# A selective-scan recurrence on one core: softplus' remainder summed on TensorE, one table set for Ln and Exp, six GpSimd drives for seven

## What is computed

```python
dt = softplus(x_dbl[..., :dt_rank] @ W_dt.T + b_dt)      # (B, 1024, 128)
A = -exp(A_log)                                          # (128, 16)
def step(h, inp):
    dt_t, B_t, C_t, u_t = inp
    dA = exp(dt_t[..., None] * A)
    h = dA * h + (dt_t * u_t)[..., None] * B_t[:, None, :]
    return h, einsum('bdn,bn->bd', h, C_t)
y = ys + u * D_skip
return y * silu(z) @ W_out.T
```

## Time and profile before

| what | us |
|---|---|
| median of the three runs | 741.99 |
| lowest and highest run | 741.06, 745.93 |
| span of the profiled execution, first to last instruction | 740.9 |
| median less that span | 1.1 |
| the units, from the first drive to the last product | 45.0 to 473.0 |

### The profile page before, as it was taken

The page is one execution under the profiler, slowest core; times in us unless marked ns, Lnnn a source line. Parts: engine busy times, 40 slices in busy tenths (PEclk is TensorE's granted clock), DMA queues, the critical chain, the costliest instruction groups (busy, mean ns, idle before and its releaser), DMA issues.

```text
span 740.9 us, 10581 instructions
## 1 busy us (share of the span) xinstructions
PE 605.2 (82%) x3591; PEld 253.3 (34%) x3591; DVE 571.3 (77%) x589; ACT 440.8 (59%) x662; POOL 470.9 (64%) x250
## 2 busy tenths in 40 slices
PE   4876696797896787987777788898889988999997
PEld 2321121121221211221212122245656335777762
DVE  4489999998998998998998999554465545666645
ACT  3887767668587578578577555163545515555532
POOL 6369999999999999999999999650000310000002
PEclk9999789789998998998998999999999999999999
DMA  3389566577576666666675675000000000000001
GB/s 99 85 275 306 227 230 234 199 254 236 201 256 233 210 243 237 223 232 229 207 260 198 242 244 199 21 0 1 3 4 9 1 19 1 2 1 2 2 2 60
DMA packets 33112, 105.35 MB, mean 142 GB/s; under 512 B 6933, under 2 KB 7454, under 8 KB 33054
## 3 DMA queue, kind: packets, MB, share of 16 engines
q1 hardware_dynamic: 31958, 103.94, 41.1%
q10 hardware_dynamic: 776, 0.55, 0.3%
q0 software_dynamic: 320, 0.13, 0.1%
HBM read 98.84 MB, written 2.10 MB: 136 GB/s over the span
## 4 chain that ended last, share of the span: by engine, by line
PE 41%; POOL 16%; DVE 16%; issue 15%; ACT 7%; DMA 3%; DVEq 0%; SPq 0%; POOLq 0%; ACTq 0%
POOL hc L1764 8%; POOL dbu L1775 8%; DVE hh_all L1464 7%; PE py L229 6%; PE pb L198 6%; PE px L252 5%; PE py L727 5%; DVE pb L1459 4%; DMA cc<-scr 2%; PE pb L939 2%; PE px L754 2%; PE pb L715 1%; PE py L963 1%; PE px L242 1%; DVE yg L1473 1%
## 5 line engine op out<-in xcount | busy, mean ns | idle before, releaser
L1764 POOL TENSOR_TENSOR hc<-hh_all,cc 128x1024 f32<-128x1024 f32 x128 | 300.2, 2390 | 2.4 <-DVE hh_all L1464 1.3
L727 PE MATMUL py<-hc,w_cst 64*64 64x512 f32 x1024 | 153.2, 658 | 26.9 <-POOL hc L1764 17.1
L1464 DVE TENSOR_TENSOR_SCAN hh_all<-da,pb 128x1024 f32<-128x1024 f32 x72 | 164.6, 2286 | 2.5
L1778 POOL TENSOR_TENSOR yg<-w_xs 128x512 f32<-128x512 f32 x10 | 12.6, 1266 | 232.6 <-DVE w_xs L1599 142.8
L1464 DVE TENSOR_TENSOR_SCAN hh_all<-pb,dbu 128x1024 f32<-128x1024 f32 x56 | 127.7, 2280 | 17.4 <-POOL dbu L1775 13.9
L1775 POOL TENSOR_TENSOR dbu<-bb,dtu_all 128x1024 f32<-128x1024 f32 x56 | 133.8, 2389 | 0.0
L715 PE MATMUL pb<-bc,w_sel 128*128 128x512 bf16 x144 | 48.2, 420 | 66.1 <-DVE hh_all L1464 63.6
L1184 ACT ACTIVATE pb<-dt_all,w_aneg 128x1024 f32<-128x1024 f32 x56 | 62.6, 1118 | 58.5 <-DVE hh_all L1464 56.9
L1459 DVE TENSOR_TENSOR pb<-pb,dtu_all 128x1024 f32<-128x1024 f32 x72 | 87.5, 1215 | 1.9 <-DVE dtu_all L1445 0.2
L286 DVE TENSOR_REDUCE gate_all<-pb 128x1 f32<-128x1024 f32 (+7 forms) x64 | 60.4, 985 | 29.6 <-PE pb L208 14.9
L1184 ACT ACTIVATE da<-dt_all,w_aneg 128x1024 f32<-128x1024 f32 x72 | 80.5, 1137 | 0.5
(11 more groups left out here) (291 smaller groups left out, 950.3 us busy)
## 6 DMA issues: line engine op xcount, KB each, us to landing
cc<-scr SPq DMA_DIRECT2D x128, 512.0 KB, 4.5
bb<-scr SPq DMA_DIRECT2D x56, 512.0 KB, 4.8
w_xs<-hc SPq DMA_DIRECT2D x6, 256.0 KB, 4.6
w_xst<-in_x SPq DMA_DIRECT2D x2, 512.0 KB, 5.4
scr<-bcf SPq DMA_DIRECT2D x8, 128.0 KB, 3.8
w_xs<-dt_all SPq DMA_DIRECT2D x4, 256.0 KB, 6.1
w_xs<-dtu_all SPq DMA_DIRECT2D x4, 256.0 KB, 5.8
out<-yg SPq DMA_DIRECT2D x4, 256.0 KB, 2.6
```

The lines of the kernel that those rows point to most:

```text
L727: last = nc.tensor.matmul(py[part(t), half(r)], ident[part(r), part(r)], hc[u % NHC][part(r), half(t)], start=(n == 0), stop=(n == NS - 1) ...
L1464: nc.vector.tensor_tensor_scan(hh[u % NHH][:, :], decay[:, :], drive[:, :], 0.0, ALU.mult, ALU.add).then_inc(scan_done, 1)
L1764: nc.gpsimd.tensor_tensor(hc[u % NHC][:, :], hh[u % NHH][:, :], cc[u % NCC][:, :], ALU.mult).then_inc(hc_done, 1)
```

## The change

The remainder of softplus leaves VectorE for all sequences but the first. For those, ScalarE's Ln no longer overwrites `px[h]`, but goes to `dt`; TensorE adds 1 to -(1+e) by four matmuls of one row by 128 columns of ones, and then adds `dt`, `ex` and `rl` by identity matmuls. Ln waits for ScalarE's own step instead of VectorE's. After the gate at n = 2 ScalarE loads the table set that has both Ln and Exp. One of seven pooled states of each sequence becomes an own state, and the list is spaced anew.

```diff
-        POOLED = (1, 4, 6, 8, 10, 12, 14)
+        POOLED = (1, 4, 7, 9, 12, 14)
...
+        ones = w["sel"][0:1, 0, :]
...
         def pe_dt_add(pe, s, h):
             pe.wait_ge(ln_done, 2 * s + h + 1)
+            if s:
+                for t in range(4):
+                    nc.tensor.matmul(px[h][:, t * 128:t * 128 + 128], ones, ones, start=False, stop=False, skip_group_check=True)
+                nc.tensor.matmul(px[h][:, :], ident, dt[s % 2][:, half(h)], start=False, stop=False, skip_group_check=True)
             nc.tensor.matmul(px[h][:, :], ident, ex[:, half(h)], start=False, stop=False, skip_group_check=True)
             nc.tensor.matmul(px[h][:, :], ident, rl[:, half(h)], start=False, stop=True,
                              skip_group_check=True).then_inc(px_full[h], 1)
...
         def act_ln(act, s, h):
-            act.wait_ge(lost_done, 2 * s + h + 1)
-            nc.scalar.activation(px[h][:, :], px[h][:, :], ACT.Ln, scale=-1.0).then_inc(ln_done, 1)
-
-        def act_dt_out(act, s, h):
-            act.wait_ge(px_full[h], full(s, ADD))
-            atleast(act, scan_done, NS * (s - 1))
+            if s == 0:
+                act.wait_ge(lost_done, h + 1)
+            else:
+                act.wait_ge(one_done, 2 * s + h + 1)
             if s == 1:
                 for v in (4, 6):
                     act.wait_ge(xs_in[v], 32)
+            nc.scalar.activation(dt[s % 2][:, half(h)] if s else px[h][:, :], px[h][:, :], ACT.Ln, scale=-1.0).then_inc(ln_done, 1)
+
+        def act_dt_out(act, s, h):
+            act.wait_ge(px_full[h], full(s, ADD))
             nc.scalar.activation(dt[s % 2][:, half(h)], px[h][:, :], ACT.Copy).then_inc(dt_done, 1)
...
+                if n == 2 and q < LAST:
+                    act.preload_act_table_set("natural_log_exp_and_others")
                 if q == LAST:
                     act_first_pair(act, n)
...
                     if q < LAST:
-                        if n == 9 + h:
-                            dve_lost(dve, q + 1, h)
                         if n == 11 + h:
                             dve_dtu(dve, q + 1, h)
```

## The result

The kernel after takes 753.6 us (median of four runs, 750.5 to 755.8), the kernel before beside it 741.5; the ratio is 1.015, with an interval of 1.011 to 1.018. The forecast was 737.0, the range 727 to 748: the change was to bring a little time, and it costs some.

The account below looks back on a forecast made before the run. GpSimd was taken to set the pace at 53.15 us a sequence; 52.4 after saves 5.2, less 1.2 in sequence 0, plus 0.8 at the end: 4.8 off the 740.9 span, 736.1, median 737, range 727 to 748.

Parts of the forecast that it names:

- GpSimd's part: GpSimd's work per sequence: one drive fewer takes off 2.31 us, leaving 22 x 2.31 = 50.84 us.
- VectorE's part: VectorE's work per sequence: 1.24 us more for the own state, 1.16 less for the remainders, giving 50.43 us.
- The chain to Ln: ScalarE's list from the end of scan 7 to the end of Ln of half 0: 9.1 us.
- The four matmuls of one row: TensorE's four additions with one row of weights and 128 columns: 0.3 us together.
- Half 1: TensorE's additions for the second half of the next dt: 3.24 us, as for half 0.
- The new wait: VectorE's product with u waits for ScalarE's copy: 0.5 us for half 0, 1.1 for half 1, 1.6 a sequence.
- the sum: A sequence takes 50.4 + 0.4 + 1.6 = 52.4 us against 53.15; the units take 419.4 us.
- Half 0 costs 3.24 and is done at 12.4: TensorE's additions for half 0 take 3.24 us and end 12.4 us after scan 7.
- its second rival: TensorE's clock is at half in the additions: at 1.5 us a sequence the time is 747; chance 0.20.
- Sequence 0: Loses 1.2 us: GpSimd's product waits for the C row's DMA, and state 7's drive stands three operations behind.
- GpSimd's drives x48, 54.9 us: Sign in the profile: GpSimd's drives x48, 54.9 us, in place of x56.
- The load at n = 2: ScalarE's added table load: two loads a sequence, not four; their removal taken at nothing more than its place in the chain.

Follow-up runs that it names:

- both_fill: Kernel after, with zero-weight matmuls on TensorE at two places: six ahead of state 8's B row, eight ahead of the wait for half 0's Ln; 738.0 us.
- dt_fill: Kernel after, with six zero-weight matmuls on TensorE ahead of state 8's B row; 741.4 us.
- loads_only: Kernel before, with only the added load at n = 2 of the table set holding Ln and Exp; 744.0 us, ratio 1.001.
- early_no_load: Kernel after, with Ln reading e and the ones, e and relu added ahead of Ln's wait, but without the table load at n = 2; 743.6 us.
- clock_fill: Kernel after, with eight zero-weight matmuls on TensorE ahead of its wait for Ln of half 0; 741.6 us.
- early_old_fill: Kernel after, with additions ahead of Ln's wait, the old list of seven pooled states and eight zero-weight matmuls ahead of half 0's additions; 751.0 us.

## Why the prediction was wrong

**What held.** GpSimd's part: 50.77 us of work (50.84 predicted), idle time before its products instead of waits for its drives, and 50.7 us periods once the chain is hidden. VectorE's part: 50.10 (50.43). The chain to Ln: 9.0 us (9.1) where the projection is not late, without table loads. The four matmuls of one row: 0.32 us (0.3). Half 1: 3.16 (3.24). The new wait: VectorE's product with u for ScalarE's copy, and it decides. With the clock held up at both places (projection and half 0's additions at 1.00 in all seven sequences) the sum held for the units, 419.0 us against 419.4 (both_fill).

**The step that failed** is "Half 0 costs 3.24 and is done at 12.4". It took 4.55 to 4.87 us in six of seven sequences, since TensorE's clock fell from 1.00 to 0.50 on the way. The prediction knew this as its second rival and put it at 0.20, with the argument that TensorE's gaps there would be "1.1, 0.6 and 1.7 us, none as long as 2.4". The 2.4 is the 2.38 us of the earlier trace rows ahead of state 11's B row, where the stretch at 0.50 of the earlier trace rows begins. That fails twice. In sequences 2 to 5 the last gap was 2.25 to 2.74 us. And in sequences 1 and 6 the gaps came out as forecast, and the clock fell all the same, 1.6 and 1.1 us after TensorE had gone back to work. The mistake was to read from two rows of before that gaps shorter than 2.4 us are safe, when the trace of before had seven cases to count. From the first to the last of half 0's two additions, in sequences 1, 2 and 4 (clock in the column before the DMA share):

```profile
132.91:135.81 2.90, 2.90 (x4) 1.11 (x5) 2.87 (x4) 2.07 (x3) 2.90 (x3) 0.65 0.67 216
186.08:188.00 1.92, 1.92 (x4) 0.68 (x4) 1.92 (x3) 1.08 (x2) 1.92 (x2) 0.99 0.67 218
292.47:295.80 3.33, 3.33 (x5) 1.17 (x5) 3.30 (x4) 2.48 (x3) 3.33 (x3) 0.57 0.58 198
```

In the kernel before the clock was already low in half 0's additions in six sequences of seven (2.3 to 3.8 us at a mean of 0.87 to 0.50, instead of 2.0), and it cost nothing there, as GpSimd set the pace (VectorE waited 0.2 us for the copy in all). All seven had a gap of 1.9 to 2.4 us some 3 us ahead, the one at full clock too (2.38): the length of a gap doesn't tell. So 0.20 was far too low for this rival. Its time of 747 adds 1.5 us a sequence. No run shows that term as such, nor the spread whose middle ends the range and whose upper part has the chance of 0.08; what the runs showed in its place is 9.5 us over six sequences in half 0's additions, 1.6 each, so the price was about right. The 747 falls short of the 753.6 by the next point, by the 4.4 us behind the last scan, and by the 3 us from the profiled execution to the median, less what the start and sequence 0 gave back.

**A term that was missing**: the list change also moves an idle time of 3.01 us to the place before state 8's B row, and slows the projection behind it: 2.06 to 3.58 us in sequences 2 to 5, at a mean granted clock of 0.95 to 0.55, where 1.98 were taken at 1.00. The prediction followed what the list does to GpSimd, VectorE and ScalarE, but on TensorE only as far as the additions. ScalarE waited 4.5 us for it, and dt_fill removes that; of its 12 us, the profile shows 7.6 in the units, from this and from two sets of additions that became fast.

**Sequence 0** was to lose 1.2 us. Its period fell from 52.0 to 50.8: the C row's DMA held GpSimd 1.52 us once, and the later drive of state 7 was hidden; the one drive that VectorE waited for, 1.1 us, was state 9's.

**A wrong figure.** "GpSimd's drives x48, 54.9 us" among the signs can't be right: 48 drives of 2.39 us are 114.7, and 113.5 were measured. Nothing rests on it.

**The load at n = 2** "at nothing more than this" held for the loads in number and place: two a sequence. What they are worth depends on the bound: nothing that can be told while GpSimd sets the pace (loads_only), 16 us when the chain does (early_no_load).

The parts, put together from the runs: the shorter list alone loses 0.5%, the common table set alone changes nothing that can be told (0.999 to 1.003), the new softplus and table set with the old list lose 0.7%, all of them lose 1.5%, and all of them with the additions ahead of Ln's wait win 2.1%. Not settled: why the old list with the early additions is 3 to 4 us above the kernel before, why the stretch of attention differs by up to 5 us between profiles, and what decides in which sequence the clock falls: after equal gaps it fell in some and not in others.

## What to carry to other kernels

When work moves to TensorE behind a wait, price it at both clock levels (1.00 and 0.50 here), and count in the whole trace how often each one was granted, rather than reading a safe gap from one or two rows; list TensorE's idle times over the whole stretch that a reordering touches, not only at the edit. Then look which addends don't depend on what is waited for: issued ahead of the wait they leave the chain and give TensorE work where it stood idle, and here that made the difference between 753.6 and 727.4 us. Filling with empty matmuls brought 15.6 of these 26.2 us, and in these runs it helped where TensorE stood idle: where it didn't, it cost time (3.5 us in sequence 0 of clock_fill, 5.0 in early_old_fill).

## What was not expected of the hardware

- The clock fell during work. After gaps of 1.07, 0.66 and 1.62 us between short matmuls, TensorE ran 1.62 us of additions at a granted clock of 1.00, and was at 0.50 for the next 2.9 us: the fall came in the midst of matmuls.
- Equal gaps, different clocks: in dt_fill the last gap ahead of half 0's additions was 1.7 us in six sequences, and the clock fell in four of them (mean 0.65 to 0.69) and stayed at 1.00 in two.
- Four bf16 matmuls with one row of weights and 128 columns cost 0.32 us, 0.08 each, at a granted clock of 1.00 (kernel after, 127.88 to 128.20).
